# Sums over the states in batches of three column groups, in a selective-scan and attention kernel on one core

## The chip, the cores and the metric

The kernel runs on one core of one Trainium2 chip. The metric is the device time of one execution in microseconds (us); lower is better. In the trace the engines are PE (TensorE matmuls), PEld (TensorE weight loads, which overlap the matmuls), DVE (VectorE), ACT (ScalarE), POOL (GpSimd) and SP (the engine that issues the DMAs).

## The reference, cut to what matters

An input of 4 images x 16 x 16 x 192 goes through a state-space block, then linear attention, then an attention over 6 chosen heads of 12. The change touches only the scan of the first block:

```
def step(h, inp):                       # 256 steps in sequence
    u_t, d_t, B_t, C_t = inp            # per image and direction (4 directions)
    dA = jnp.exp(d_t[..., None] * As)   # 96 channels x 16 states
    h = h * dA + (d_t * u_t)[..., None] * B_t[:, :, None, :]
    y = jnp.einsum('bkcn,bkn->bkc', h, C_t)
    return (h, y)
```

The last line sums over the 16 states of each channel. The y of the four directions are then brought back to one order and added.

## The kernel before, in words

The 4 images are two halves of 2. A scan `n` (0 to 7) is one half in one direction. It has 96 channels x 16 states x 512 positions; 8 channels x 16 states fill the 128 partitions, so a scan is 12 **units** and the whole is 96 units (`SLOT_COUNT`). A unit `u` takes these steps, each engine in its own written order:

- PE, `spread_out(u)`: two bf16 matmuls (L1310 into `step_bc`, L1314 into `inp_bc`) spread the 8 channels over their 16 states each. There are two buffers of each. The first waits for the decay of unit u-2, the second for the scan of unit u-2.
- ACT, `expo(u)`, L690: the decay, from `step_bc`.
- DVE, `drive_of(u)`, L939, multiplies `inp_bc` by B, and `scan(u)`, L948, runs the recurrence into one of four `state` slots.
- POOL, `weigh(u)`, L528: `outp` = state x C, into one of three `outp` slots (`SLOTS`), so it waits for the sum of unit u-3 (`y_mm`).
- PE, `sum_states`, L1323: a float32 matmul with the 0/1 matrix `band` (128 x 96) adds the 16 states of each channel into `y_acc`, 96 x 512 in one PSUM bank. All 12 units of a scan accumulate into the same bank, each with zeros for the 88 channels that it does not hold. Each such matmul appears in the trace as two, so 96 sums are 192 rows.
- DVE, `add_y(n)`, L963, L966 or L973: at unit 3 of the next scan `y_acc` is added to `y_sum`; it waits for the sums of all 12 units.

PE's order in the loop at step u is `spread_out(u + 1)`, `sum_states(u - 3)`, then `pre` of a coming scan once in 12 steps (L1300), then the side products of the step. Side products are weight preparation in steps 14 to 42 and, from step 52 on, the attention work of the first half of the images, while the scans of the second half run (steps 48 to 95). After the last unit come `sum_states` of the last three units, `add_y(7)`, and then `rest`, the attention of what is left, which has no scan in it.

The stationary matrix of the sum is a window of `band`:

```
at = DI - GRP - GRP * g12
t_.matmul(y_acc[0:DI, :], band[:, at:at + DI], outp[:, u % SLOTS, :], ...)
```

Constants: `DI` 96, `GRP` 8, `UNITS` 12, `CHUNK` 32, `CHUNKS` 3, `PER_CHUNK` 4, `DIRS` 4.

Of the kernel before, what the change touches and what calls it, by code (L numbers as in the profile page):

```python
# [24 lines left out]
P = 128  # L25
# [4 lines left out]
TOK = IMG * L  # L30
TILES = TOK // P
CK = CH // 2
DI, NS, RANK, DIRS = 96, 16, 12, 4
GRP = P // NS
UNITS = DI // GRP
CHUNK = 32
CHUNKS = DI // CHUNK
PER_CHUNK = CHUNK // GRP
# [6 lines left out]
RING = 3  # L45
SLOTS = 3
STATE_SLOTS = 4
Y_LAG = 3
SOFTPLUS_LINEAR = 40.0
SERIES_BELOW = 0.0025  # L50
# [17 lines left out]
SLOT_COUNT = SCANS * UNITS  # L68
# [61 lines left out]
def products(step, n):  # L130

    if step in NO_PRODUCT:
        return []
    if step in WEIGHT_STEPS:
        return [step]
    if step[0] == "h" and step[1:].isdigit():
        j = int(step[1:])
        return [f"pt{n}{j - 2}"] * (1 < j <= TOPK + 1) + [f"pv{n}{j - 3}"] * (j > 2) + [f"s{n}{j}"] * (j < TOPK)
    return [f"{step}_{n}"]


def preparing(u, at):
# [27 lines left out]
def hybrid_kernel(nc, x, in_proj_w, conv_w, conv_b, x_proj_w, dt_w, dt_b, A_logs, Ds, norm_g, norm_b, out_proj_w,  # L170
# [5 lines left out]
    with ExitStack() as ctx:  # L176
        ctx.enter_context(nc.allow_non_contiguous_dma(reason="small parameter vectors"))

        def sb(name, shape, dt=F32):
            return ctx.enter_context(nc.sbuf_tensor(name, shape, dt))  # L180
# [30 lines left out]
        y_acc = ctx.enter_context(nc.psum_tensor("y_acc", [P, TOK], F32))  # L211
# [19 lines left out]
        band = sb("band", [P, 2 * DI - GRP])  # L231
# [44 lines left out]
        c_rep = sb("c_rep", [P, 2, TOK])  # L276
# [15 lines left out]
        n = TILES * CH  # L292
# [15 lines left out]
        decay = sb("decay", [P, SLOTS, IMG, L])  # L308

        state = sb("state", [P, STATE_SLOTS, TOK])  # L310
        outp = sb("outp", [P, SLOTS, TOK])
        y_sum = sb("y_sum", [DI, TOK])
        mst = sb("mst", [P, 4, TILES, 6])
        mv = sb("mv", [P, 4, TILES, 2])
# [122 lines left out]
        def _(pool):  # L437
            g = nc.gpsimd
# [14 lines left out]
            at = NS * (DI - GRP)  # L453
# [66 lines left out]
            def weigh(u):  # L520

                n, g12 = u // UNITS, u % UNITS
                if g12 == 0:
                    pool.wait_ge(S["c_there"], 16 * GRP * (n + 1))
                pool.wait_ge(S["state"], u + 1)
                if u >= SLOTS:
                    pool.wait_ge(S["y_mm"], u - SLOTS + 1)
                g.tensor_tensor(outp[:, u % SLOTS, :], state[:, u % STATE_SLOTS, :], c_rep[:, n % 2, :],  # L528
                                ALU.mult).then_inc(S["outp"], 1)

            def side(step, n):
# [37 lines left out]
        def _(act):  # L569
# [114 lines left out]
            def expo(u):  # L684

                act.wait_ge(S["bc_step"], u + 1)
                if u >= SLOTS:
                    act.wait_ge(S["state"], u - SLOTS + 1)
                at = u % (DIRS * UNITS)
                a.activation(decay[:, u % SLOTS, :, 1:L],  # L690
                             step_bc[u % 2][:, :].rearrange("p (b l) -> p b l", b=IMG)[:, :, 1:L],
                             ACT.Exp, scale=a_neg[:, at:at + 1]).then_inc(S["decay"], 1)
# [117 lines left out]
        def _(dve):  # L810
# [131 lines left out]
            def scan(u):  # L942

                dve.wait_ge(S["drive"], u + 1)
                dve.wait_ge(S["decay"], u + 1)
                if u >= STATE_SLOTS:
                    dve.wait_ge(S["outp"], u - STATE_SLOTS + 1)
                v.tensor_tensor_scan(state[:, u % STATE_SLOTS, :], decay[:, u % SLOTS, :, :].rearrange("p b l -> p (b l)"),  # L948
# [242 lines left out]
        def _(pe):  # L1191
            t_ = nc.tensor
# [109 lines left out]
            def spread_out(u):  # L1302

                n, g12 = u // UNITS, u % UNITS
                j, q = g12 // PER_CHUNK, g12 % PER_CHUNK
                if g12 == 0:
                    pe.wait_ge(S["stack"], 16 * 9 * (n + 1))
                if u >= 2:
                    pe.wait_ge(S["decay"], u - 1)
                t_.matmul(step_bc[u % 2][:, :], spread[:, q, :], stack[:, n % 2, j, 0:TOK], start=True, stop=True  # L1310
                          ).then_inc(S["bc_step"], 1)
                if u >= 2:
                    pe.wait_ge(S["state"], u - 1)
                t_.matmul(inp_bc[u % 2][:, :], spread[:, q, :], stack[:, n % 2, j, TOK:2 * TOK], start=True, stop=True  # L1314
                          ).then_inc(S["bc_inp"], 1)

            def sum_states(u):
                n, g12 = u // UNITS, u % UNITS
                pe.wait_ge(S["outp"], u + 1)
                if g12 == 0 and n > 0:  # L1320
                    pe.wait_ge(S["y_ev"], n)
                at = DI - GRP - GRP * g12
                t_.matmul(y_acc[0:DI, :], band[:, at:at + DI], outp[:, u % SLOTS, :],  # L1323
                          start=(g12 == 0), stop=(g12 == UNITS - 1)).then_inc(S["y_mm"], 1)

            def scores(n, j):
                p = n % IMG
# [181 lines left out]
            for u in range(SLOT_COUNT):  # L1509
                if u + 1 < SLOT_COUNT:  # L1510
                    spread_out(u + 1)
                if u >= Y_LAG:
                    sum_states(u - Y_LAG)
                if preparing(u, PRE_RAW):
                    pre(preparing(u, PRE_RAW))
                for item in beside[u]:
                    side(*item)
            for u in range(SLOT_COUNT - Y_LAG, SLOT_COUNT):
                sum_states(u)
            pe.wait_ge(S["y_ev"], SCANS)  # L1520
            for item in rest:
                side(*item)
# [29 lines left out]
```

## Time and profile before

| | |
|---|---|
| median of 3 runs | 508.72 us (507.52 to 510.63) |
| profiled execution, its own time | 506.69 us |
| span of its instructions | 504.8 us |
| busy: PE, DVE | 399.8 us (79%), 379.4 us (75%) |
| busy: POOL, ACT, PEld | 199.1 us, 182.3 us, 221.4 us |
| mean granted TensorE clock | 0.839 of full speed |

The scans run from about 50 to 328 us of the span. A busy share is of the whole span; the stretches differ, so it is read by stretch. A matmul's duration in the trace is that of the pipelined instruction; what it costs PE is the distance from its start to that of the next one.

### The profile page before, as it was taken

What the parts mean: (1) busy time and instruction counts of PE and PEld (TensorE: products, weight loads), DVE (VectorE), ACT (ScalarE), POOL (GpSimd) and SP (SyncE); (2) the same over time, 40 slices, a digit from 0 to 9 for tenths busy, and PEclk for the clock granted to TensorE, in tenths of its full rate; (3) what the DMA queues carried; (4) which work ended last, traced back from release to release, by engine and by line L of the source; (5) the groups of instructions that cost most, each with busy time, mean ns of one, the idle gap of its engine ahead of it and who ended that gap; (6) DMA issues with size and microseconds to landing.
All of it is one profiled execution on the core that took longest, in us unless ns stands there. A gap on an engine that the chain in (4) does not pass through costs nothing. (4 is left out here: it accounts for less than half of the span.)

```text
span 504.8 us, 5418 instructions
## 1 busy us (share of the span) xinstructions
PE 399.8 (79%) x1545; PEld 221.4 (44%) x1545; DVE 379.4 (75%) x732; ACT 182.3 (36%) x442; POOL 199.1 (39%) x199
## 2 busy tenths in 40 slices
PE   5511485878796856959999988999999999889882
PEld 4300121224232312415466465456665849676541
DVE  6354799998999999999789899885376364353574
ACT  2253443346463633522433323233324220334340
POOL 4414585658586866754454644510010010000011
PEclk9555787769897988857999999965999996958987
DMA  6403120110112111111010100000000000000000
GB/s 132 76 5 72 44 59 12 45 31 13 45 38 53 31 40 35 26 33 32 16 42 23 26 0 1 0 2 0 2 16 2 0 0 17 1 0 1 1 16 16
DMA packets 15742, 12.66 MB, mean 25 GB/s; under 512 B 7280, under 2 KB 11362, under 8 KB 15714
## 3 DMA queue, kind: packets, MB, share of 16 engines
q1 hardware_dynamic: 15713, 12.33, 10.6%
q8 instruction: 12, 0.20, 0.2%
q14 instruction: 17, 0.13, 0.1%
HBM read 2.62 MB, written 0.79 MB: 7 GB/s over the span
## 5 line engine op out<-in xcount | busy, mean ns | idle before, releaser
L528 POOL TENSOR_TENSOR outp<-state,c_rep 128x512 f32<-128x512 f32 x96 | 128.8, 1346 | 93.7 <-PE y_acc L1323 50.0
L948 DVE TENSOR_TENSOR_SCAN state<-decay,inp_bc 128x512 f32<-128x512 f32 x96 | 117.2, 1221 | 6.7 <-DVE inp_bc L939 3.2
L1323 PE MATMUL y_acc<-outp,band 128*96 128x512 f32 x192 | 114.1, 681 | 7.2 <-DVE y_sum L963 3.2
L690 ACT ACTIVATE decay<-step_bc,a_neg 128x510 f32<-128x510 f32 x96 | 64.9, 683 | 57.8 <-PE step_bc L1310 57.6
L939 DVE TENSOR_TENSOR inp_bc<-b_rep,inp_bc 128x512 f32<-128x512 f32 x96 | 65.4, 681 | 9.9 <-PE inp_bc L1314 9.8
L472 POOL TENSOR_TENSOR rs<-mv,neg_half 128x2 f32<-128x2 f32 x16 | 11.3, 706 | 152.0 <-DVE mv L984 149.8
L1314 PE MATMUL inp_bc<-stack,spread 96*128 96x512 bf16 x96 | 42.1, 439 | 36.6 <-DVE state L948 36.3
L1310 PE MATMUL step_bc<-stack,spread 96*128 96x512 bf16 x96 | 40.9, 426 | 16.9 <-DMA stack<-lo 14.3
L1323 PEld LDWEIGHTS y_acc<-outp,band 128*96 128x96 f32 x192 | 35.1, 187 | 24.3 <-issue 10.4
L1314 PEld LDWEIGHTS inp_bc<-stack,spread 96*128 96x128 bf16 x96 | 9.9, 103 | 78.2 <-DVE state L948 72.3
L1310 PEld LDWEIGHTS step_bc<-stack,spread 96*128 96x128 bf16 x96 | 10.5, 110 | 38.4 <-issue 30.3
L710 ACT ACTIVATE prob<-ring,nmaxs 128x256 f32<-128x256 f32 x24 | 11.1, 469 | 37.0 <-DVE nmaxs L1054 37.0
L678 ACT CAST hi<-step 96x512 bf16<-96x512 f32 x16 | 9.9, 616 | 33.4 <-DVE step L918 24.9
L518 POOL TENSOR_TENSOR lo<-step,mid 96x512 bf16<-96x512 f32 x16 | 19.4, 1232 | 3.4 <-ACT mid L682 3.4
L1411 PE MATMUL ring<-kvw,tT 96*128 96x480 f32 (+1 forms) x44 | 19.7, 570 | 0.0
L1062 DVE TENSOR_SCALAR prob<-prob,prec 128x256 f32<-128x256 f32 x48 | 16.7, 389 | 0.8
L1300 PE MATMUL ring<-room_g,pre_w 96*128 96x512 f32 x16 | 11.0, 780 | 7.5 <-DVE room_g L873 7.5
L1405 PE MATMUL ring<-tT,qw 96*128 96x256 f32 (+1 forms) x64 | 15.6, 386 | 0.0
L1405 PEld LDWEIGHTS ring<-tT,qw 96*128 96x128 f32 (+1 forms) x64 | 12.3, 194 | 5.3 <-issue 4.0
L682 ACT CAST mid<-step 96x512 bf16<-96x512 f32 x16 | 9.9, 616 | 13.1 <-DVE step L931 12.9
L867 DVE SCALAR_TENSOR_TENSOR room_e<-room_w,cw,room_e 96x544 f32<-96x544 f32 x16 | 14.2, 886 | 0.5
L511 POOL TENSOR_SCALAR sps<-spe 96x512 f32<-96x512 f32 x8 | 5.2, 652 | 23.6 <-ACT spe L669 23.6
(376 smaller groups left out, 709.4 us busy)
## 6 DMA issues: line engine op xcount, KB each, us to landing
b_rep<-bc SPq DMA_DIRECT2D x64, 32.0 KB, 2.0
c_rep<-bc SPq DMA_DIRECT2D x64, 32.0 KB, 2.0
stack<-hi SPq DMA_DIRECT2D x24, 64.0 KB, 2.0
stack<-mid SPq DMA_DIRECT2D x24, 64.0 KB, 2.0
stack<-lo SPq DMA_DIRECT2D x24, 64.0 KB, 2.0
x_tok<-in_x_dram SPq DMA_DIRECT2D x2, 384.0 KB, 3.8
out_dram<-room_g SPq DMA_DIRECT2D x4, 192.0 KB, 2.0
room_a<-in_L_attn_w_qkv_dram SPq DMA_DIRECT2D x1, 432.0 KB, 6.5
```

The source lines that it names most:

```text
L518: g.tensor_tensor(lo[:, i, :], step2[:, i, :], mid[:, i, :], ALU.subtract).then_inc(S["lo"], 1)
L528: g.tensor_tensor(outp[:, u % SLOTS, :], state[:, u % STATE_SLOTS, :], c_rep[:, n % 2, :], ALU.mult).then_inc(S["outp"], 1)
L690: a.activation(decay[:, u % SLOTS, :, 1:L], step_bc[u % 2][:, :].rearrange("p (b l) -> p b l", b=IMG)[:, :, 1:L], ACT.Exp, scale=a_neg[:, ...
L867: v.scalar_tensor_tensor(sums, window, cw[:, i:i + 1], sums, ALU.mult, ALU.add).then_inc(S["conv"], 1)
L939: v.tensor_tensor(inp_bc[u % 2][:, :], b_rep[:, n % 2, :], inp_bc[u % 2][:, :], ALU.mult).then_inc(S["drive"], 1)
L948: v.tensor_tensor_scan(state[:, u % STATE_SLOTS, :], decay[:, u % SLOTS, :, :].rearrange("p b l -> p (b l)"), inp_bc[u % 2][:, :], 0.0, AL ...
L1062: v.tensor_scalar(prob[p][:, m % 2, q, :], prob[p][:, m % 2, q, :], prec[p][:, m % 2, q:q + 1], None, ALU.mult).then_inc(S["prob_divided"] ...
L1310: t_.matmul(step_bc[u % 2][:, :], spread[:, q, :], stack[:, n % 2, j, 0:TOK], start=True, stop=True).then_inc(S["bc_step"], 1)
L1314: t_.matmul(inp_bc[u % 2][:, :], spread[:, q, :], stack[:, n % 2, j, TOK:2 * TOK], start=True, stop=True).then_inc(S["bc_inp"], 1)
L1323: t_.matmul(y_acc[0:DI, :], band[:, at:at + DI], outp[:, u % SLOTS, :], start=(g12 == 0), stop=(g12 == UNITS - 1)).then_inc(S["y_mm"], 1)
L1405: ins = t_.matmul(b_[:, u * L:(u + 1) * L], qw[0:CK + c, c, i * P:(i + 1) * P], tT[0:CK + c, c, at0:at0 + L], start=(c == 0), stop=(c == 1))
L1411: ins = t_.matmul(b_[:, 0:w], tT[0:CK + c, c, at:at + P], kvw[0:CK + c, c, j, :], start=(c == 0), stop=(c == 1))
```

## The change

A unit no longer takes the next 8 channels in order. Unit `u` of a scan takes group `j = u % 3` of 32 channels and within it the part `q`, so three units in succession belong to the three groups. The three units are summed together in every third step, and each sum writes only its own 32 rows of `y_acc` (partitions 0 to 31, 32 to 63 or 64 to 95), with a window of `band` of 32 columns. The batch for units 0 to 2 comes in step 5, that of units 3 to 5 in step 8, and so on; the last one follows the loop. `outp` has five slots. The column of `a_neg` that the decay uses follows the new order.

```diff
+OUT_SLOTS = 5
+def chunk_of(u):
+    return u % CHUNKS, u % UNITS // CHUNKS
...
-        outp = sb("outp", [P, SLOTS, TOK])
+        outp = sb("outp", [P, OUT_SLOTS, TOK])
...
-                if u >= SLOTS:
-                    pool.wait_ge(S["y_mm"], u - SLOTS + 1)
-                g.tensor_tensor(outp[:, u % SLOTS, :], state[:, u % STATE_SLOTS, :], c_rep[:, n % 2, :],
+                if u >= OUT_SLOTS:
+                    pool.wait_ge(S["y_mm"], u - OUT_SLOTS + 1)
+                g.tensor_tensor(outp[:, u % OUT_SLOTS, :], state[:, u % STATE_SLOTS, :], c_rep[:, n % 2, :],
...
-                at = u % (DIRS * UNITS)
+                j, q = chunk_of(u)
+                at = u // UNITS % DIRS * UNITS + j * PER_CHUNK + q
...
-                j, q = g12 // PER_CHUNK, g12 % PER_CHUNK
+                j, q = chunk_of(u)
...
-            def sum_states(u):
-                n, g12 = u // UNITS, u % UNITS
-                pe.wait_ge(S["outp"], u + 1)
-                if g12 == 0 and n > 0:
-                    pe.wait_ge(S["y_ev"], n)
-                at = DI - GRP - GRP * g12
-                t_.matmul(y_acc[0:DI, :], band[:, at:at + DI], outp[:, u % SLOTS, :],
-                          start=(g12 == 0), stop=(g12 == UNITS - 1)).then_inc(S["y_mm"], 1)
+            def sum_states(first):
+                pe.wait_ge(S["outp"], first + CHUNKS)
+                if first % UNITS == 0 and first > 0:
+                    pe.wait_ge(S["y_ev"], first // UNITS)
+                for u in range(first, first + CHUNKS):
+                    j, q = chunk_of(u)
+                    at = DI - GRP - GRP * q
+                    t_.matmul(y_acc[CHUNK * j:CHUNK * (j + 1), :], band[:, at:at + CHUNK], outp[:, u % OUT_SLOTS, :],
+                              start=(q == 0), stop=(q == PER_CHUNK - 1)).then_inc(S["y_mm"], 1)
...
-                if u >= Y_LAG:
-                    sum_states(u - Y_LAG)
+                if u % CHUNKS == CHUNKS - 1 and u >= Y_LAG:
+                    sum_states(u - Y_LAG - CHUNKS + 1)
...
-            for u in range(SLOT_COUNT - Y_LAG, SLOT_COUNT):
-                sum_states(u)
+            sum_states(SLOT_COUNT - CHUNKS)
```

## Rows read from the trace of the kernel before

**Rows 1.** Windows by stage: us, busy (instructions) by engine, PEclk, DMA.

```profile
57.00:108.00 51.00, 34.12 (x73) 11.02 (x74) 50.13 (x61) 18.80 (x32) 33.50 (x25) 0.79 0.16 39
108.00:120.00 12.00, 12.00 (x40) 5.75 (x39) 10.19 (x13) 8.53 (x17) 8.12 (x10) 0.76 0.07 16
120.00:228.00 108.00, 80.94 (x221) 29.55 (x220) 105.48 (x147) 48.07 (x85) 74.96 (x61) 0.85 0.16 38
228.00:330.00 102.00, 96.33 (x413) 56.15 (x412) 90.24 (x138) 34.44 (x79) 49.59 (x41) 0.97 0.07 16
330.00:505.00 175.00, 154.35 (x728) 106.18 (x728) 96.00 (x317) 51.66 (x191) 12.25 (x16) 0.84 0.02 5
```

**Rows 2.** Windows of 12 us in the stretch where PE is full, same columns.

```profile
228.00:240.00 12.00, 12.00 (x39) 7.09 (x38) 11.33 (x14) 3.66 (x6) 6.19 (x6) 0.78 0.10 24
240.00:252.00 12.00, 12.00 (x36) 5.58 (x35) 9.36 (x13) 5.52 (x11) 4.88 (x5) 1.00 0.07 16
252.00:264.00 12.00, 12.00 (x59) 8.16 (x58) 11.10 (x14) 3.58 (x9) 7.15 (x6) 1.00 0.20 44
264.00:276.00 12.00, 12.00 (x58) 7.66 (x57) 10.96 (x18) 4.61 (x9) 4.72 (x4) 1.00 0.08 19
276.00:288.00 12.00, 12.00 (x43) 5.97 (x41) 10.66 (x20) 3.74 (x8) 8.27 (x8) 1.00 0.13 33
288.00:300.00 12.00, 11.42 (x76) 8.00 (x75) 10.79 (x21) 3.94 (x10) 5.08 (x4) 1.00 0.00 0
300.00:312.00 12.00, 8.92 (x54) 5.35 (x54) 11.76 (x22) 3.47 (x13) 4.88 (x4) 1.00 0.00 1
312.00:324.00 12.00, 11.15 (x48) 6.59 (x47) 9.55 (x14) 4.90 (x13) 5.25 (x5) 1.00 0.00 0
324.00:330.00 6.00, 4.84 (x13) 1.74 (x14) 4.73 (x10) 1.02 (x4) 3.16 (x3) 1.00 0.00 0
```

**Rows 3.** The same windows for L1323 alone: PE and PEld busy, PEclk, DMA.

```profile
228.00:330.00 102.00, 38.02 (x72) 11.42 (x70) 0.97 0.07 16
```

**Rows 4.** Costliest groups: busy, mean ns, idle before, releaser.

```profile
L528 POOL TENSOR_TENSOR outp<-state,c_rep 128x512 f32<-128x512 f32 x96 | 128.8, 1346 | 93.7 <-PE y_acc L1323 50.0
L948 DVE TENSOR_TENSOR_SCAN state<-decay,inp_bc 128x512 f32<-128x512 f32 x96 | 117.2, 1221 | 6.7 <-DVE inp_bc L939 3.2
L1323 PE MATMUL y_acc<-outp,band 128*96 128x512 f32 x192 | 114.1, 681 | 7.2 <-DVE y_sum L963 3.2
L939 DVE TENSOR_TENSOR inp_bc<-b_rep,inp_bc 128x512 f32<-128x512 f32 x96 | 65.4, 681 | 9.9 <-PE inp_bc L1314 9.8
```

**Rows 5.** Chain of waits, pieces in order of time: start, us, what.

```profile
323.03 0.86 PE y_acc L1323 x2
...
384.98 0.98 PE ring L1349 x4
385.96 1.06 PE ring L1331 x4
```

**Rows 6.** Timeline at half clock: start, us, engine, line.

```profile
84.22 1.91 PE L1323 MATMUL y_acc<-outp,band 128*96 128x512 f32 x2
...
85.93 0.63 PE L1310 MATMUL step_bc<-stack,spread 96*128 96x512 bf16 x1
...
86.36 0.63 PE L1314 MATMUL inp_bc<-stack,spread 96*128 96x512 bf16 x1
```

**Rows 7.** Timeline at the end of the scans, same columns.

```profile
324.88 3.85 PE L1323 MATMUL y_acc<-outp,band 128*96 128x512 f32 x8
324.96 1.22 DVE L948 TENSOR_TENSOR_SCAN state<-decay,inp_bc 128x512 f32<-128x512 f32 x1
325.08 2.49 POOL L528 TENSOR_TENSOR outp<-state,c_rep 128x512 f32<-128x512 f32 x2
...
328.76 0.58 DVE L973 TENSOR_TENSOR y_sum<-y_sum,y_acc 96x256 f32<-96x256 f32 x1 [1.17 <-PE y_acc L1323]
```

**Rows 8.** One line of DVE: duration min/median/max, first and last start.

```profile
L931 DVE TENSOR_TENSOR step<-step,hi x16: 660/662/1450, 40.8 to 273.3; 96x512 f32<-96x512 f32 x16
```

**Rows 9.** Waits in the stretch of 228 to 330 us: total, times, longest.

```profile
POOL outp L528 <- PE y_acc L1323: 36.7, 21, 3.3
```

## The prediction

> **What bounds the kernel now.** I read the windows by stage first [rows 1], because the shares of the whole span hide that the limits differ. From 57 to 228 us (about 60 of the 96 units) DVE is busy 165.8 of 171 us, while PE is busy 127 of 171: DVE sets the pace, at 171/60 = 2.85 us a unit. From 228 to 330 us, where the attention work of the first half stands beside the last 36 units, PE is busy 96.3 of 102 us and DVE 90.2: there PE sets the pace most of the time. After 330 us there is no scan, and the change touches no instruction. The finer windows [rows 2] show how much room DVE leaves in the PE-bound stretch: DVE's idle time, 12 minus its busy time, is 0.67, 2.64, 0.90, 1.04, 1.34, 1.21, 0.24 and 2.45 us, and 1.27 in the last 6 us, in all 11.8 us. That is the most that any relief of PE can give in the scans, since no DVE work is removed. The costliest groups [rows 4] name PE's part in it: L1323 with 114.1 us busy. In the PE-bound stretch it has 38.0 us and 72 matmuls [rows 3], which are 36 sums or 12 batches of three.
>
> **The sum itself.** At full clock one sum takes PE 0.86 us, two matmuls of 0.43 [rows 5]; at half clock 85.93 - 84.22 = 1.71 us, two of 0.85 [rows 6]. I call one such matmul a slot. A batch of three sums is 6 slots one after another: 2.58 us. The change keeps 6 matmuls of 512 columns, narrows their output from 96 to 32 rows, and puts the three sums on different groups of rows. Narrowing alone gives nothing: four matmuls of L1349, 32 rows and 256 columns wide, take 0.98 us, and four of L1331, 128 rows and 256 columns, take 1.06 [rows 5]. A gain must come from sums of different groups running at the same time, and no row shows two such neighbours, so I bound it from both sides. Lower end: the three run fully side by side, 2 slots. Upper end: none overlaps, 6 slots. In between, if matmuls start only in written order and the second matmul of a sum must wait for the first, which uses the same rows, then the second of one sum can run only beside the first of the next: 4 slots. Going in and out of the narrow shape has a price too: the four slots of L1349 at 256 columns should take 4 x 0.213 = 0.85 us and take 0.98, the four of L1331 0.21 more; I take 0.2 a batch, between 0.1 and 0.35. So a batch costs 2 x 0.427 + 0.2 = 1.06 us, or 4 x 0.427 + 0.2 = 1.91, or 2.78, against 2.58.
>
> The Trainium skill bears on this. "TensorE: Matmul & The Clock Gate", Part 3, states that matmuls to different column tiles overlap and gives 2.38 times for three tiles of 512 columns; by that a batch would take 2.58/2.38 = 1.08 us, an estimate. The same part states that matmuls start and end in program order. By that the first case becomes the second, as worked out above from slots, since each float32 sum is two matmuls on one tile. "TensorEngine Tiling (Array Packing)", Key Properties, states that a change of tiling mode drains the engine; the 0.1 to 0.2 us at L1349 and L1331 agree with it. No run so far shows any overlap.
>
> **Part by part, against the profiled execution.**
>
> PE-bound stretch, 12 batches. With 4 slots each saves 0.67 us, 8.0 us in all or 0.94 per 12 us; it counts only as far as DVE has idle time, so window by window the smaller of the two: 0.67 + 0.94 + 0.90 + 0.94 + 0.94 + 0.94 + 0.24 + 0.94 + 0.47 = 7.0. With 2 slots it saves 1.52, or 2.1 per 12 us: 0.67 + 2.1 + 0.90 + 1.04 + 1.34 + 1.21 + 0.24 + 2.1 + 1.05 = 10.7. DVE does not become fully busy even where it is the bound; there about 0.2 us per 12 remain, so 1.7 us are taken off: gains of 5.3 and 9.0 us.
>
> DVE-bound stretch, 20 batches. The average load of PE falls, and that gives nothing. What can cost is the lump. In a batch step PE issues `inp_bc` of unit u+1 when scan u-1 ends, then the batch, then both spreads of u+2, and DVE wants the second of them two units later, on average 5.7 us. At full clock this path is 0.2 + 1.91 + 0.2 + 0.4 = 2.7 us and hidden. At half clock it is 0.43 + 3.42 + 0.2 + 0.43 + 0.63 = 5.1 us with 4 slots [slot lengths from rows 6]: just hidden, but in some 8 of the 20 steps a weight product or `pre` stands behind the batch, which adds 1.6 us at half clock and leaves DVE 1.0 us short. The granted clock of 0.79, 0.76 and 0.85 [rows 1] means half clock in about 35% of this stretch, so 8 x 1.0 x 0.35 = 2.8 at most; I take 1.2 us. With 2 slots: nothing.
>
> Moved and added waits. The first sum of a scan now stands two steps after `add_y`, so PE's waits for `y_sum` (3.2 us at L963, [rows 4]) go; where DVE or its cap is the bound this gives nothing more. `add_y` itself now waits for a batch in the same step in which the single sum stood; it is 1.0 us later with 4 slots, 0.2 with 2, and PE's work behind it goes on, so it costs only at the end. There the last `outp` is done at 325.08 + 2.49 = 327.57 us and DVE starts the last `add_y` 1.19 later, at 328.76 [rows 7], behind one sum; now behind three: +1.0 us with 4 slots, +0.2 with 2. The batch before it (units 90 to 92) fits ahead of that time. The index changes, the five slots and the column of `a_neg` cost nothing: same instructions, and the slot count for POOL lets it start earlier.
>
> POOL. Its 36.7 us of waiting for sums in the PE-bound stretch [rows 9] mostly vanish, so `weigh` starts right at the end of each scan instead of some 2 us later. POOL is no bound (busy 49.6 of 102). But a DVE instruction that reads only SBUF sometimes takes longer: L931 has 0.66 as median and 1.45 as its longest [rows 8], and in that instance POOL's L528 was running. With POOL moved, such meetings move too: +-2 us, taken at 0, because some of the present ones go.
>
> Sum with 4 slots: -5.3 + 1.2 + 1.0 = -3.1 us; with 2 slots: -9.0 + 0.2 = -8.8 us. The profiled execution is 506.7 us, 2.0 below the median of 508.7, so on the scale of the median: 505.6 and 499.9. **My forecast is that the groups overlap at least in part, and as no row leans to one end I take the middle of the two, -6 us, about 503.**
>
> **Rivals.**
> 1. *Written order halves the overlap* (4 slots): 505.6 us. For it: each sum is two matmuls on the same rows, which the 192 rows for 96 sums show. Against it: nothing in the trace. It is the upper part of my forecast, and it decides between a measurable gain and none.
> 2. *No overlap, and the lump stalls DVE*: slower. A batch is 2.78 us at full clock, 5.3 at half. PE-bound stretch: 12 x 0.2 = +2.4. DVE-bound stretch at half clock: 0.43 + 5.3 + 0.43 + 0.63 = 6.8 against 5.7, 1.1 x 20 x 0.35 = +7.7. End: +1.9. Together +12, 520.7 us, and about 514 if DVE catches up half of it. Its place is the start of DVE's L939 after each batch step; it decides from where a batch at half clock costs more than 5.7 - 1.5 = 4.2 us, about 5 slots. For it: no row of overlap, and L1349's 32-row matmuls save nothing by themselves.
> 3. *The clock takes it back*. A less loaded PE may be granted half clock in the PE-bound stretch, which now has 0.97 [rows 1]. One window of 12 us at 0.5 instead of 1.0 costs about 6 us there, since its products double: about 508.5 us, no change. Against it: with 2 slots PE still has over 80 of 102 us of work. The same place holds the meetings of POOL and DVE of above, if they turn out at +2 or worse.
>
> **How the numbers follow.** Overlap in part or in full 0.70, of which 4 slots 0.38 and 2 slots 0.32; no overlap 0.17; gain lost to clock or meetings 0.13. The range of 498 to 512 holds the first group nearly whole (499.9 and 505.6, each with about 2 us for the POOL meetings and the clock) and the third, and reaches towards rival 2; the overlap group alone would be 498 to 507.5. One per cent, about what a measurement of this kernel can tell from no change, is 5.1 us: faster is below 503.6, slower above 513.8. Faster: 0.30 of the 2-slot case, 0.13 of the 4-slot case, 0.03 of the rest, 0.46. Slower: most of rival 2 and a little of the third, 0.18. Within: 0.36.
>
> **What the profile after would show.** The distance from the start of a batch to PE's next instruction: 1.06, 1.9 or 2.8 us at full clock tells the slots at once. DVE's busy time in the last 36 units should rise towards 11.8 of 12. POOL's waits for `y_acc` should be near zero. In the first 60 units DVE's waits for `inp_bc` L1314 should stay near zero; if they appear at half clock, rival 2 or the lump of the 4-slot case is at work. The last `add_y` should start 1.4 us (2 slots) or 2.2 us (4 slots) after the last `outp`. The prediction would be wrong if PE's clock in the PE-bound stretch falls below 0.9, or if DVE's SBUF-only instructions grow by more than 2 us in total.

## The result, and the profile after

The changed kernel takes 523.49 us (median of 4 runs, 521.72 to 533.3) beside 509.68 for the kernel before on the same chip (4 runs): ratio 1.0274, interval 1.0205 to 1.0343. It is slower by about 14 us, where 503 had been forecast. Some executions of every version are a few per cent longer than the rest: medians here are over all runs, ratios over the fast ones alone, and as the execution profiled first was a slow one (533.3 us), the rows below are from a second profile of the same kernel, experiment e1. That execution took 524.18 us, span 522.3; the median of e1 over 4 runs is 522.5 (517.79 to 524.18), ratio 1.0266, interval 1.0203 to 1.033. The change adds lines, so numbers shift: L1332 is L1323 of the kernel before, L1321 is L1314, L946 is L939, L955 is L948 and L534 is L528.

The windows by stage answer to [rows 1]:

```profile
57.00:108.00 51.00, 28.81 (x70) 5.24 (x69) 48.61 (x57) 18.77 (x33) 33.23 (x25) 0.58 0.17 39
108.00:120.00 12.00, 8.54 (x17) 2.39 (x18) 11.42 (x15) 4.71 (x9) 6.41 (x9) 0.50 0.07 16
120.00:228.00 108.00, 72.66 (x233) 22.99 (x231) 101.22 (x141) 48.75 (x88) 74.14 (x62) 0.71 0.15 36
228.00:330.00 102.00, 90.56 (x383) 53.03 (x382) 87.59 (x130) 33.17 (x73) 48.16 (x38) 0.78 0.08 18
```

The column to read is PEclk: 0.79, 0.76 and 0.85 have become 0.58, 0.50 and 0.71, and in the PE-bound stretch 0.97 has become 0.78. PE is busy there for 90.56 us, only 5.8 less than before, and DVE for 87.59 us, where it had 90.24. As the scans of e1 end 13 us later, the window holds less of their work (383 matmuls of PE beside 413). The same work lies between the start of the recurrence (L948, here L955) of unit 60 and that of unit 95, the last; before, then e1:

```profile
215.18:324.96 109.78, 100.04 (x418) 57.52 (x419) 99.06 (x151) 36.31 (x80) 53.58 (x45) 0.92 0.08 20
222.34:338.05 115.71, 98.19 (x421) 56.83 (x421) 100.04 (x151) 35.95 (x80) 55.05 (x45) 0.79 0.08 19
```

At full clock 12 batches are some 19 us shorter than 36 single sums (12 x (2.58 - 0.99), the 0.99 from below). PE's busy time fell by 1.9 us, at a granted clock of 0.79 instead of 0.92.

The groups of PE that answer to [rows 4] and to its L1314:

```profile
L1332 PE MATMUL y_acc<-outp,band 128*32 128x512 f32 x192 | 50.7, 881 | 3.1 <-POOL outp L534 3.1
L1321 PE MATMUL inp_bc<-stack,spread 96*128 96x512 bf16 x96 | 48.4, 505 | 56.5 <-DVE state L955 56.2
```

The 192 matmuls of the sums keep PE busy for 50.7 us instead of 114.1, at the lower clock, so the relief is there, and larger than half. But L1321, which the change doesn't touch, has a mean of 505 ns, between the 0.38 and 0.63 us that single ones take at the two levels of the clock.

One batch at full clock and one at half clock, from the timeline of PE (start, us), answer to [rows 5, 6]:

```profile
249.12 0.38 PE L1321 MATMUL inp_bc<-stack,spread 96*128 96x512 bf16 x1
249.43 1.06 PE L1332 MATMUL y_acc<-outp,band 128*32 128x512 f32 x6
250.42 1.13 PE L1307 MATMUL ring<-room_g,pre_w 96*128 96x512 f32 x2
...
67.68 1.93 PE L1332 MATMUL y_acc<-outp,band 128*32 128x512 f32 x6
69.54 0.61 PE L1317 MATMUL step_bc<-stack,spread 96*128 96x512 bf16 x1
```

From the start of a batch to PE's next instruction are 250.42 - 249.43 = 0.99 us at full clock and 69.54 - 67.68 = 1.86 at half: three sums, six matmuls, in little more than the 0.86 and 1.71 us of one sum. The three groups of rows run side by side.

Where the time went is read from the starts of the recurrences on DVE, 12 units at a time; "last scan" is here the recurrence of unit 95. For before and for e1, in us:

| stretch | before | e1 | difference |
|---|---|---|---|
| span's start to first scan | 50.49 | 51.11 | +0.6 |
| units 0 to 11 | 36.4 | 37.1 | +0.7 |
| 12 to 23 | 37.8 | 41.8 | +4.0 |
| 24 to 59 (three times 12) | 27.1, 28.4, 35.1 | 27.4, 29.8, 35.1 | +1.8 |
| 60 to 83 (two times 12) | 40.6, 35.4 | 40.2, 36.7 | +0.9 |
| 84 to the last scan | 33.8 | 38.8 | +5.0 |
| last scan to the end | 179.8 | 184.3 | +4.5 |

Of the 5.0 us of the last twelve units 4.2 are one event: from the recurrence of unit 84 to the next pass 6.94 us, before 2.78. The timeline of e1 at this place (PE and DVE only; the last bracket is DVE's idle time before the instruction):

```profile
299.22 5.34 PE L1428 MATMUL ring<-v,room_a 128*128 128x34 f32 x24
299.24 1.22 DVE L955 TENSOR_TENSOR_SCAN state<-decay,inp_bc 128x512 f32<-128x512 f32 x1
...
304.78 0.63 PE L1321 MATMUL inp_bc<-stack,spread 96*128 96x512 bf16 x1
305.45 0.69 DVE L946 TENSOR_TENSOR inp_bc<-b_rep,inp_bc 128x512 f32<-128x512 f32 x1 [4.99 <-PE inp_bc L1321]
```

The attention product `cx` (24 matmuls, 5.34 us here, 2.76 before) runs at half clock; the `inp_bc` of the next unit is queued behind it, and DVE stands still for 4.99 us. In this event the chain is: half clock, a long product that no longer fits between two recurrences, an idle DVE.

The end of the scans in e1 answers to [rows 7]:

```profile
338.05 1.22 DVE L955 TENSOR_TENSOR_SCAN state<-decay,inp_bc 128x512 f32<-128x512 f32 x1
338.17 2.48 POOL L534 TENSOR_TENSOR outp<-state,c_rep 128x512 f32<-128x512 f32 x2
340.70 1.21 PE L1332 MATMUL y_acc<-outp,band 128*32 128x512 f32 x6 [3.07 <-POOL outp L534]
342.00 1.07 DVE L980 TENSOR_TENSOR y_sum<-y_sum,y_acc 96x256 f32<-96x256 f32 x2 [1.33 <-PE y_acc L1332]
```

The last `add_y` starts 342.00 - (338.17 + 2.48) = 1.35 us after the last product; before it was 1.19. POOL's waits from 228 to 330 us (total, times, longest), against [rows 9]:

```profile
POOL outp L534 <- DVE state L955: 29.3, 14, 5.6
POOL outp L534 <- PE y_acc L1332: 18.6, 7, 5.5
```

### The profile page after: what moved, and what is told of

It is laid out like the page before. It is cut to its first block and busy times, and to the rows that moved or that the text cites. A ratio compares the mean times of both kernels' runs of the same rounds, so it can differ in the third digit from the quotient of the medians.

```text
span 530.9 us, 5416 instructions
## 1 busy us (share of the span) xinstructions
PE 401.2 (76%) x1545; PEld 212.7 (40%) x1545; DVE 382.5 (72%) x732; ACT 181.5 (34%) x442; POOL 200.1 (38%) x199
## 3 DMA queue, kind: packets, MB, share of 16 engines
q1 hardware_dynamic: 15713, 12.33, 10.1%
## 5 line engine op out<-in xcount | busy, mean ns | idle before, releaser
L534 POOL TENSOR_TENSOR outp<-state,c_rep 128x512 f32<-128x512 f32 x96 | 130.4, 1364 | 103.4 <-DVE state L955 70.2
L955 DVE TENSOR_TENSOR_SCAN state<-decay,inp_bc 128x512 f32<-128x512 f32 x96 | 117.2, 1221 | 7.0 <-DVE inp_bc L946 3.8
L1321 PE MATMUL inp_bc<-stack,spread 96*128 96x512 bf16 x96 | 49.9, 520 | 56.0 <-DVE state L955 55.9
L946 DVE TENSOR_TENSOR inp_bc<-b_rep,inp_bc 128x512 f32<-128x512 f32 x96 | 65.4, 682 | 15.1 <-PE inp_bc L1321 15.1
L1317 PE MATMUL step_bc<-stack,spread 96*128 96x512 bf16 x96 | 48.5, 505 | 19.0 <-DMA stack<-lo 14.3
L1332 PE MATMUL y_acc<-outp,band 128*32 128x512 f32 x192 | 51.7, 898 | 3.1 <-POOL outp L534 3.1
L1321 PEld LDWEIGHTS inp_bc<-stack,spread 96*128 96x128 bf16 x96 | 10.5, 110 | 91.0 <-DVE state L955 85.0
L1317 PEld LDWEIGHTS step_bc<-stack,spread 96*128 96x128 bf16 x96 | 11.8, 123 | 47.9 <-issue 35.4
L1414 PE MATMUL ring<-tT,qw 96*128 96x256 f32 (+1 forms) x64 | 22.7, 518 | 0.0
L1307 PE MATMUL ring<-room_g,pre_w 96*128 96x512 f32 x16 | 14.1, 976 | 7.5 <-DVE room_g L880 7.5
L1414 PEld LDWEIGHTS ring<-tT,qw 96*128 96x128 f32 (+1 forms) x64 | 16.7, 266 | 6.5 <-issue 3.1
L1281 PE MATMUL ring<-room_j,room_a 96*96 96x384 f32 (+1 forms) x16 | 10.6, 763 | 5.6 <-DVE room_j L899 5.6
L664 ACT ACTIVATE step<-ring,dtb 96x512 f32<-96x512 f32 x8 | 5.5, 683 | 24.8 <-PE ring L1307 24.8
```

The costliest lines, as they stand in the source:

```text
L534: g.tensor_tensor(outp[:, u % OUT_SLOTS, :], state[:, u % STATE_SLOTS, :], c_rep[:, n % 2, :], ALU.mult).then_inc(S["outp"], 1)
L946: v.tensor_tensor(inp_bc[u % 2][:, :], b_rep[:, n % 2, :], inp_bc[u % 2][:, :], ALU.mult).then_inc(S["drive"], 1)
L1332: t_.matmul(y_acc[CHUNK * j:CHUNK * (j + 1), :], band[:, at:at + CHUNK], outp[:, u % OUT_SLOTS, :], start=(q == 0), stop=(q == PER_CHUNK - ...
L1414: ins = t_.matmul(b_[:, u * L:(u + 1) * L], qw[0:CK + c, c, i * P:(i + 1) * P], tT[0:CK + c, c, at0:at0 + L], start=(c == 0), stop=(c == 1))
```

## The experiments

The theory after the result: (A) a less loaded PE is granted a lower clock, and this takes the relief back. Rivals: (B) the lump, three sums in one step, delays `inp_bc`; (C) five slots let POOL start earlier, where its products run beside instructions of DVE on SBUF and one of the two is held up, called a meeting below; (D) the narrow form costs PE time of its own. The kernels first undo one part each.

**e1**, the changed kernel again. 

> The changed kernel again, for a profile beside the variants. The first profile had the three sums of a batch side by side (about 1.0 us a batch at full clock, 1.8 at half) but a granted clock of 0.54, 0.50, 0.71 and 0.73 where the kernel before had 0.79, 0.76, 0.85 and 0.97. Clock theory (PE has less to do in the scans, so the chip grants half clock for more of them, and the products there double): about 522 us, mean clock about 0.74. Lump theory (the batch and its wait for three outputs hold PE back, whatever the clock): the same time, but with PE standing in front of the batch or DVE waiting right after batch steps also where the clock is full.


Measured: 522.5 us, as above. Both theories had forecast this time, so it decides nothing between them.

**e2**, the batch with sums of 96 rows.

```diff
-                    at = DI - GRP - GRP * q
-                    t_.matmul(y_acc[CHUNK * j:CHUNK * (j + 1), :], band[:, at:at + CHUNK], ...
+                    at = DI - GRP - GRP * (PER_CHUNK * j + q)
+                    t_.matmul(y_acc[0:DI, :], band[:, at:at + DI], ...
```

> Order of the units, batches of three and five output slots as changed, but each sum writes all 96 rows again, so nothing runs side by side and PE has its old load. Clock theory: the clock comes back to about 0.84 and the time to 507 to 512 us. Lump theory: the lump is now 2.58 instead of 1.0 us long, so the time stays at 522 or goes above it.


Measured: 532.05 us (528.06 to 533.02, 4 runs), ratio 1.047 (1.0418 to 1.0523). The clock theory had forecast 507 to 512 us and missed: the clock did come back (0.82 and 0.90 in the two stretches, e1: 0.65 and 0.78), the time did not. So the lump without overlap is dear, and the overlap is worth 532.05 - 522.5 = 9.5 us against the same lump, at the clock that each is granted. DVE's waits in 57 to 350 us show the lump: 9.5 us for `inp_bc`, 6.5 for the softplus chain, whose product `pre` stands behind a batch, and 5.0 for `y_acc`.

**e3**, the narrow sums one at a time, a sum each step, five slots.

```diff
-                pe.wait_ge(S["outp"], first + CHUNKS)
+                pe.wait_ge(S["outp"], first + 1)
...
-                for u in range(first, first + CHUNKS):
+                for u in range(first, first + 1):
...
-                if u % CHUNKS == CHUNKS - 1 and u >= Y_LAG:
-                    sum_states(u - Y_LAG - CHUNKS + 1)
+                if u >= Y_LAG:
+                    sum_states(u - Y_LAG)
...
-            sum_states(SLOT_COUNT - CHUNKS)
+            for u in range(SLOT_COUNT - Y_LAG, SLOT_COUNT):
+                sum_states(u)
```

> Each sum writes its 32 rows, but alone, in the step in which the kernel before had it, so the sums take PE 2 slots each as before and only the width of the output is less. Clock theory by PE's busy time: clock and time as before, 508 to 512 us (plus up to 3 us for changing shape 96 times). Clock theory by the part of the array in use: the clock falls as in the changed kernel and the time is 518 us or more. Lump theory: as before, 508 to 512 us.


Measured: 521.96 us (518.79 to 529.38), ratio 1.0266 (1.0211 to 1.032), with a granted clock of 0.853 in the profile. No version of the theories had this pair: the lower time was forecast with a full clock, the higher one with a low clock. In this pair of kernels the clock goes with PE's busy time and not with the number of rows that a sum writes. The timeline of PE shows the price of the shape:

```profile
260.29 0.38 PE L1321 MATMUL inp_bc<-stack,spread 96*128 96x512 bf16 x1
260.60 1.05 PE L1332 MATMUL y_acc<-outp,band 128*32 128x512 f32 x2
261.57 1.19 PE L1428 MATMUL ring<-v,room_a 128*128 128x34 f32 x9
```

From `inp_bc` to the sum are 0.31 us, not the 0.22 that lie between two wide neighbours, and the pair takes 0.97 instead of 0.86: 0.2 us for going in and out of the narrow shape, 7 us over the 36 sums of the PE-bound stretch.

**e4**, the changed kernel with two repeated products a unit.

```diff
+                for _ in range(FILL):            # FILL = 2
+                    t_.matmul(step_bc[u % 2][:, :], spread[:, q, :], stack[:, n % 2, j, 0:TOK], start=True, stop=True)
                 t_.matmul(step_bc[u % 2][:, :], ...
```

> The changed kernel with two extra copies of the L1310 spread product in each unit, written to the same buffer just ahead of the real one and overwritten by it; this gives PE back 0.43 us a unit at full clock of the 0.53 that the change took, and nothing else. Clock theory: the clock rises towards 0.84 or above and the time falls well below 522, to 500 to 512 us, although PE does more. Lump theory: more work ahead of each decay, so 522 or slower.


Measured: 520.35 us (518.31 to 522.79), ratio 1.0257 (1.0207 to 1.0306): not to be told from e1. The filler brings the granted clock back to 0.81 before 228 us and to 0.90 behind it (e1: 0.65, 0.78), and it puts 2 x 0.22 = 0.44 us a unit on PE, of the 0.5 us that the batches had taken off. The clock was bought back with the time that had been saved. The forecast of the clock theory, 500 to 512 us, missed. And with nearly the load of the kernel before and most of its clock, e4 is still 12 us slower, so the clock can't be all of the loss: between the recurrences of units 60 and 95 it takes 114.6 us (e1 115.7, before 109.8) at a mean clock of 0.88 (0.79, 0.92).

**f1**, the kernel before with five output slots and nothing else; **f2**, the new order of units alone; **f3**, the changed kernel with three slots; **f4**, e3 with three slots.

```diff
 f1
-        outp = sb("outp", [P, SLOTS, TOK])
+        outp = sb("outp", [P, OUT_SLOTS, TOK])     # 5, in weigh and sum_states too
 f2: after.py with e3's loop, e2's matmul and OUT_SLOTS = 3
 f3: after.py with OUT_SLOTS = 3
 f4: e3 with OUT_SLOTS = 3
```

> The kernel before with five output slots in place of three and nothing else. In all variants with five slots DVE was busy 3 to 5 us longer on the same instructions, in those that read and write only SBUF. Meeting theory (POOL's product, no longer held back by the sums, meets these instructions of DVE and holds them up): DVE busy rises by 3 to 5 us over 379.4 and the time by 2 to 5 us, to 510 to 513. Clock theory alone: no change, 508.


Measured: 518.75 us (513.21 to 525.22, 6 runs) against 507.9, ratio 1.0209 (1.017 to 1.0248). More than either theory had allowed (508, or 510 to 513).

> The kernel before with the units in the new order (three groups in turn) and nothing else: single sums of 96 rows, three slots. Every theory: as before, 508 us, within 2.


Measured: 508.65 us (12 runs), ratio 1.0002 (0.9978 to 1.0025). The order costs nothing.

> The changed kernel with three output slots, so POOL waits for each batch and then makes three products in a row. Meeting theory: other meetings than with five slots, DVE busy nearer to 379 us, time 518 to 522. Lump theory: POOL stands still until each batch, scans are held by their own slots, slower than 523. Clock theory: as the changed kernel, 522, clock 0.74.


Measured: 530.7 us (529.99 to 531.11), ratio 1.0443 (1.0418 to 1.0467). With three slots POOL has to wait for the batch (108.3 us in 27 waits for `y_acc` over the run) and then computes three products in a row, beside which DVE is busy for 391.2 us, 11.8 more than before. Of the forecasts only that of the lump theory, slower than 523, holds. Beside e1 it also shows that the batch needs the slots: five of them are 8.2 us better than three here, where without a batch (f1) they are 10 us worse.

> Single sums of 32 rows in the old steps with three output slots: the narrow shape alone. The variant with five slots took 522 us and showed 0.21 us more per sum on PE at full clock (0.10 going in, 0.11 coming out). Switching theory: 36 sums in the stretch where PE is the bound x 0.2 = 7 us, little elsewhere, so 514 to 517 us, 3 to 5 below the one with five slots. If the meetings were the larger part, 510.


Measured: 514.55 us (514.39 to 525.56, 6 runs), ratio 1.0126 (1.01 to 1.0152). This is the shape alone: +6.6 us, near the 7 worked out under e3, so (D) holds for single sums; a batch pays it only once in three.

Put in a row, in medians: order +0.7, five slots +10.1 (f1 against f2), lump at full width +13.3 (e2 against f1), overlap -9.6 (e1 against e2), sum +14.5. These are steps along one path and not properties of the parts: f1 has the old order, and five slots are worth +10 without the batch and -8 with it.

The next four ask why slots cost, between a shift of buffers in SBUF and an earlier POOL.

```diff
 g1: before.py
-        outp = sb("outp", [P, SLOTS, TOK])
+        outp = sb("outp", [P, 5, TOK])             # three in use
 g2: after.py, g3: f1, g4: e4, each with
                 pool.wait_ge(S["state"], u + 1)
+                pool.wait_ge(S["bc_inp"], min(u + 2, SLOT_COUNT))
```

> The kernel before, with outp allocated for five slots but still rotated over three, so that only the places of the later buffers in SBUF change and no wait does. f1 with five slots in use cost 2.1%. Theory T (what costs is that POOL starts its product earlier, at the end of each scan, and so runs beside other DVE instructions): no change, 508 us, ratio 1.000. Rival L (the moved buffers cost): 516 to 519 us as in f1, ratio about 1.02.


Measured: 508.46 us (506.17 to 510.94, 12 runs), ratio 1.0018 (0.9994 to 1.0042). Not the places of the buffers.

> The changed kernel, with one more wait in weigh: POOL's product of unit u also waits for inp_bc of unit u+1, which PE issues just ahead of the place where the kernel before issued the sum that POOL waited for. So POOL is held back in the PE-bound stretch about as before, less one sum. Theory T: the 10.8 us that five slots cost in f1 come back at least in part, 512 to 515 us instead of 522.5, ratio about 1.01. Rival L: still 520 to 524, ratio 1.025, or above, as a later POOL makes the batches later. A second rival, that the lower clock is the larger part of the loss: also 520 to 524, with a granted clock of 0.74 to 0.78.


Measured: 526.54 us (525.09 to 537.02), ratio 1.0368 (1.0325 to 1.0412). Theory T missed, and the time is above the 520 to 524 of the other two, of which rival L had added "or above": worse than without the gate. A later POOL that makes the batches later would do this, but no row was read for it; the granted clock was 0.72.

> The kernel before with five slots in use, as f1, and the same wait of POOL for inp_bc of unit u+1. Theory T: back to 508 to 511 us, ratio 1.00 to 1.006. Rival L: 516 to 519 us, ratio 1.02.


Measured: ratio 1.0084 (1.004 to 1.0127); the 10 runs are spread over 509.48 to 525.32 us, median 516.28. By its ratio this looks like half a success of the gate, but the profile doesn't bear it out: the last scan starts at 330.44 us, in f1 at 330.23, and the granted clock of the scans is the same (0.87, 0.95). The gate changed nothing there. What differs between these two profiled executions, 509.7 and 517.3 us in span, lies at the very end, in stretches that neither kernel changes. f1:

```profile
474.00:486.00 12.00, 10.48 (x52) 6.02 (x51) 7.17 (x23) 5.74 (x22) 0.00 (x0) 1.00 0.00 0
486.00:498.00 12.00, 8.12 (x37) 4.32 (x36) 9.39 (x31) 5.25 (x18) 1.69 (x2) 1.00 0.05 16
```

and g3:

```profile
474.00:486.00 12.00, 10.48 (x33) 5.36 (x33) 4.58 (x14) 3.53 (x15) 0.00 (x0) 0.64 0.00 0
486.00:498.00 12.00, 11.95 (x38) 6.65 (x36) 7.28 (x24) 4.66 (x15) 0.92 (x2) 0.65 0.00 0
```

The first window has the same 10.48 us of PE's time for 52 matmuls in the one and 33 in the other: full clock against 0.64. That costs 186.9 - 179.5 = 7.4 us behind the last scan.

> The changed kernel with POOL's added wait of g2 and the two repeated spread products a unit of e4, which brought the granted clock from 0.74 to 0.78 up to 0.81 to 0.85. If the meetings and the clock each carry a part and add up, this is the sum of both: 522.5 - 2 (e4) - 8 to 10 (g2 by theory T) = 510 to 512 us, ratio about 1.006. If neither carries it, 520, ratio 1.025.


Measured: 526.42 us (520.74 to 533.54), ratio 1.0315 (1.0261 to 1.0369). That is above both forecasts (510 to 512, and 520). The parts don't add up to a gain; with g2 this ended the idea that a held-back POOL repairs the change.

The last four ask where the slots' time lies, and whether relief of PE has any worth.

```diff
 h1: f1 again, for a second profile
 h2: before.py, h3: f1, each with
+                w = TOK if g12 == 0 else TOK // 4
-                t_.matmul(y_acc[0:DI, :], band[:, at:at + DI], outp[:, u % SLOTS, :],
+                t_.matmul(y_acc[0:DI, 0:w], band[:, at:at + DI], outp[:, u % SLOTS, 0:w],
 h5: e4
-                for _ in range(FILL):
+                for _ in range(FILL if u < 60 else 0):
```

> The kernel of f1 once more (the kernel before with five output slots), for a second profile. If the five slots cost in the scans, the last scan starts at 330 us as in f1's and g3's profiles and what varies is the part behind it: 179.5 us with PE at full clock about 150 us behind the last scan, 187 us with half clock there. If the slots' cost lies elsewhere, the scans end 5 us or more later than 330 in a run of 516 us or more.


Measured: 525.3 us in one execution, span 523.5. The last scan starts at 333.73 and the rest takes 189.8 us: the span is 13.8 us longer than in f1's profile, of the same kernel. 10.3 us more lie behind the scans, and 4.5 in the last twelve units, where the event of e1 stands again:

```profile
300.40 0.70 DVE L940 TENSOR_TENSOR inp_bc<-b_rep,inp_bc 128x512 f32<-128x512 f32 x1 [4.54 <-PE inp_bc L1315]
```

So that event needs no batch and no narrow rows, and no relief of PE either; half clock at this place is enough: in f1's profile, the same program with full clock there, the wait is 0.69 us.

> The kernel before, with 11 of every 12 sums cut to a quarter of their 512 columns (so three quarters of the columns lack all but the first unit's sum). Order, waits, slots and the 96 rows are as before; PE is relieved by about 0.6 us a sum, 20 us in the last 36 units, the same as by the overlapped batches. If relief of PE is worth what the prediction said for 2 slots: -9, about 499 us, ratio 0.982, last scan 9 us earlier. If the clock takes it back: a granted clock of 0.75 to 0.80 against 0.84 to 0.88, and 506 to 510 us.


Measured: 515.52 us (one run at 507.41, the other five from 515.30 to 516.86) against 508.44 (shortest run 506.7). The forecast for worthwhile relief had been 499, that of the clock theory 506 to 510. Whether it is slower at all can't be said from two groups of runs; that it isn't faster can. The granted clock is low in all six, 0.72 to 0.78. Its windows by stage:

```profile
57.00:108.00 51.00, 28.58 (x72) 11.81 (x72) 49.87 (x57) 20.24 (x35) 34.59 (x26) 0.57 0.17 40
108.00:120.00 12.00, 8.66 (x24) 4.17 (x24) 11.74 (x15) 5.89 (x11) 6.41 (x9) 0.53 0.07 17
120.00:228.00 108.00, 69.05 (x231) 34.48 (x229) 103.39 (x143) 48.60 (x87) 76.95 (x62) 0.67 0.16 37
228.00:330.00 102.00, 92.85 (x410) 66.31 (x410) 90.29 (x135) 34.55 (x78) 48.21 (x39) 0.76 0.07 17
```

These are the clearest rows of the study. Order, waits, slots, rows and step of every sum are those of the kernel before; only PE's work is less, by some 20 us in the last stretch. The clock falls to 0.57, 0.53, 0.67 and 0.76, PE is busy for 92.85 us instead of 96.33, and DVE does 90.29 us of work where it did 90.24. From the recurrence of unit 60 to that of unit 95 h2 takes 110.8 us (331.34 - 220.56), 1.0 more than before, where 9 less had been forecast. So (A) is shown for the clock, and for the gain that did not come, without the help of any other part of the change.

The same trace, unit by unit against before, shows how. From unit 65 to unit 71, where both have full clock but for the first microsecond, h2 takes 16.5 us instead of 19.8: while the clock stays, relief does count. Units 73, 74 and 84, at half clock in the main, then lose 3.9 us. The largest piece, 2.4 us in unit 84, is the event of e1, with neither batch nor five slots:

```profile
295.50 5.17 PE L1420 MATMUL ring<-v,room_a 128*128 128x34 f32 x24
301.56 0.69 DVE L939 TENSOR_TENSOR inp_bc<-b_rep,inp_bc 128x512 f32<-128x512 f32 x1 [3.26 <-PE inp_bc L1314]
```

Another 2.4 us go in units 71 and 81, and not by the clock: there instructions of DVE on SBUF last longer, L909 1.40 us and the two of L991 0.95, with a product of POOL beside them. f1 and e1 lose the same 2.3 us in these two units. L909 before, then in h2 with POOL's product:

```profile
253.26 1.09 DVE L909 SCALAR_TENSOR_TENSOR spl<-spe,spl 96x512 f32<-96x512 f32 x1
...
255.36 2.49 DVE L909 SCALAR_TENSOR_TENSOR spl<-spe,spl 96x512 f32<-96x512 f32 x1
256.04 1.27 POOL L528 TENSOR_TENSOR outp<-state,c_rep 128x512 f32<-128x512 f32 x1
```

The units from 87 on gain 1.9 us again, which leaves the 1.0.

> The same short sums with five output slots. If relief is worth its 9 us and the slots cost 10.8 as in f1: 510 us. If the clock takes the relief back: 518 us, ratio 1.02. If the slots cost because POOL starts earlier, they cost nothing here beyond h2, as with short sums POOL no longer waits long for a slot in either kernel: h3 equals h2.


Measured: 514.5 us (510.26 to 522.47, 12 runs), ratio 1.0102 (1.0064 to 1.014), clock 0.717 to 0.784. Neither 510 nor 518; by the medians five slots add nothing to h2, but both spread too widely to say more. In its profile units 60 to 95 take 108.5 us, 1.3 less than before.

> The changed kernel with two repeated spread products a unit in units 0 to 59 alone, where DVE sets the pace. If the low clock there makes the scans late (half-clock batches and weight products in the steps of 2.85 us): 516 to 518 us, since e4's filler is kept where it helps and left out where it costs PE time. If the clock of the last 36 units matters instead: 522 as the changed kernel. e4, with filler in all units, had 520.4.


Measured: 522.23 us (518.57 to 527.15), ratio 1.0241 (1.0198 to 1.0285): the changed kernel's time. Clock 0.78 before 228 us and 0.77 behind it. In its first 60 units it gains 2.4 us on e1, and the last twelve take 38.8 us as there. The forecast by a lower clock in the first 60 units, 516 to 518 us, missed. That the clock of the last 36 units decides instead is not shown: e4, which has it back at 0.90, takes 38.6 us for the same twelve.

The mean granted clock of all profiled executions in the two stretches goes with PE's load:

| kernels | PE's load | 57 to 228 us | 228 to 330 us |
|---|---|---|---|
| before, g1, f1 and h1, f2, f4, g3, e3, e2 | full-length sums, one after another | 0.82 to 0.87 | 0.90 to 0.98 |
| e4, g4 | overlapped sums and filler | 0.81, 0.78 | 0.90, 0.88 |
| h5 | overlapped sums, filler in the first 60 units | 0.78 | 0.77 |
| the changed kernel (first profile and e1), f3, g2 | overlapped sums | 0.61 to 0.65 | 0.73 to 0.78 |
| h2, h3 | short sums | 0.63 | 0.76, 0.80 |

No version is faster than the kernel before.

## Why the prediction was wrong

**The bound.** Right as a reading of the state before, wrong as a base for a sum. That PE sets the pace in the last 36 units assumed that its work has a fixed length.

**The sum itself.** The overlap was foreseen, with 4 slots as the likelier case; what came is the 2 slots: 0.99 us a batch at full clock, or 1.08 with the 0.09 that PE takes longer going in, where 1.06 had been worked out. Written order doesn't halve the overlap, though each sum is two matmuls on the same rows; rivals 1 and 2 fall, as far as they rest on missing overlap. The rule of the Trainium skill that gives 2.38 times for three column tiles ("TensorE: Matmul & The Clock Gate", Part 3) agrees with this trace: 2.58/1.08 is 2.4, and 2.58/0.99 is 2.6. The other rule of that part, on starts and ends in program order, is not contradicted by these rows, but it does not cost the 4 slots that the prediction worked out beside it. The 0.2 us for the shape was right too (0.2 in e3).

**The PE-bound stretch**, forecast -9.0 us, is the step that failed. Between the starts of scan 60 and the last scan e1 takes 40.2 + 36.7 + 38.8 = 115.7 us against 109.8, +5.9. The failed assumption is the one beside rival 3, that "PE still has over 80 of 102 us of work" and so keeps its clock; it had 90.56 and was granted 0.78. (With 2 slots the prediction's own numbers give less than 80: 96.3 - 12 x 1.52 = 78.1.) Rival 3's mechanism is what the runs showed, and its price for one window, about 6 us, was fair (4.2 for the event at 299 us). Its extent was not: one window of 12 us had been counted, and 0.78 means half clock in (1 - 0.78)/0.5 = 44% of 102 us. h2, with this clock and no other part of the change, has +1.0 us in place of the -9: what full clock gave in some units went back at half clock (3.9 us) and in the meetings of DVE with POOL (2.4). Rival 3 had been given 0.13, for no change; how the other 5 us of e1 divide among clock, lump and slots is not shown. The event of unit 84 is half clock in e1 and in h1 (39.1 us for the last twelve units), but e4 takes as long there with half clock only from 310 to 320 us, in five waits of DVE for `inp_bc`, of which three (1.44, 0.65 and 1.87 us) stand at full clock.

**The DVE-bound stretch**, nothing forecast for 2 slots: +6.5 us in the first 60 units. It isn't the stall that had been feared in the place where it had been feared; from unit 1 on, DVE's waits for `inp_bc` L1321 are all behind 299 us. But the lump does reach DVE by another way, the softplus chain, whose product `pre` stands behind a batch:

```profile
74.40 1.93 PE L1332 MATMUL y_acc<-outp,band 128*32 128x512 f32 x6
...
76.26 2.08 PE L1307 MATMUL ring<-room_g,pre_w 96*128 96x512 f32 x2
...
79.09 0.42 DVE L912 TENSOR_SCALAR spl<-step 96x512 f32<-96x512 f32 x1 [1.59 <-ACT step L664]
```

Besides a first one near 54 us that all these versions have, e1 has three such waits in this stretch, 2.9 us in all, at half clock in the main. The kernel before has none, nor has h2 with the low clock but no lump, nor e4 with the lump and a clock of 0.81. Of the rest, 2.4 us are more work of DVE in units 12 to 23, in SBUF-only instructions beside POOL, and 1.3 a longer wait of L886 for its input from ACT (3.38 us at half clock, 2.09 before).

**POOL.** "Taken at 0" was wrong, and so was "the five slots cost nothing". The same DVE instruction in g1 and in f1, with POOL's beside it:

```profile
117.61 0.83 DVE L905 TENSOR_SCALAR spl<-step 96x512 f32<-96x512 f32 x1
118.11 1.47 POOL L528 TENSOR_TENSOR outp<-state,c_rep 128x512 f32<-128x512 f32 x1
```

```profile
119.61 2.08 DVE L906 TENSOR_SCALAR spl<-step 96x512 f32<-96x512 f32 x1
120.11 1.29 POOL L529 TENSOR_TENSOR outp<-state,c_rep 128x512 f32<-128x512 f32 x1
```

Both pairs start 0.50 us apart in the records. In g1 DVE is through in 0.83 us and POOL's product is the longer one; in f1 DVE lasts until 121.69, 0.3 us beyond POOL's end. The Trainium skill ("SBUF — State Buffer", "SBUF: two separate sides") calls the port pair of the two an exclusive lock for a whole instruction, which goes to the one that starts first. These rows agree in that one lasts until about the other's end; they don't bear out the second half as recorded: in both pairs DVE's start is the first, and only in f1 is DVE held up. DVE's busy time over the whole run is 3.1 us above before's 379.4 in e1, 5.3 in f1 and 11.8 in f3. But f2, with three slots, has 2.5 as well and costs nothing in its median, and its units 12 to 23 take the same 40.2 us as f1's. So f1 has some 3 us more of such meetings than f2, not ten, and they don't explain the difference of the medians.

**Behind the scans** nothing had been forecast, since no instruction changes: +4.5 us in e1. In the profiles of this kernel family this part has anything from 179.1 us (f2, mean clock 0.85) to 190.8 us (the first profile of the changed kernel, 0.80). So the end of the scans can move and the total by more or less than that.

**The signs.** Right: the batch's length; no waits for `inp_bc` in the first 60 units; the last `add_y` 1.35 us after the last product (1.4). Wrong: DVE busy for 10.3 of 12 us in 228 to 330 us, not near 11.8; POOL's waits for `y_acc` halved (18.6 us), not gone. Both conditions under which the prediction called itself wrong came true: the clock below 0.9, and SBUF-only work of DVE up by more than 2 us.

**Left open.** Why five slots alone move f1's median by 10 us. Three profiles put 3.5 to 9 us of it before the last scan (330.23, 330.44 and 333.73 us against 324.96 and 326.72 for before and g1) and 0 to 10 behind it, at half clock; but f2's profile has its last scan at 329.74 as well. That the slots make half clock behind the scans more likely is what the medians suggest, and no run here shows the way in which they would. How much of e1's 14.5 us each of lump, slots and clock would carry alone can't be told either, since they act through the same clock: the differences between the medians are known to about 3 us each.

## What to carry to other kernels

Before counting relief of PE as time, read its granted clock in that stretch and ask what the engine does with less work: here about two thirds of the sums' work was removed twice, by overlap and by leaving columns out, and each time the clock fell and most of the gain went back with it. A cheap check is the second of these: cut the columns of the matmuls that an idea would save, change nothing else, and see if the kernel becomes faster at all. And more slots for a buffer are a change of timing, to be tried alone.

## What the runs showed of the hardware

- Three groups of float32 sums, each two matmuls on 32 rows of their own, issued one sum after the other, take 0.99 us at full clock and 1.86 at half; one sum of 96 rows takes 0.86 and 1.71.
- A single sum in the narrow shape costs about 0.1 us on the way in and 0.1 on the way out (e3), +6.6 us for 96 sums (f4).
- With the sums' load cut to a third, the mean granted clock fell from 0.83 to 0.63 or 0.65 in 57 to 228 us, and from 0.97 to 0.76 or 0.78 in 228 to 330 us, though PE was busy there for 90 us and more of 102 (e1, h2; e2, with batches of full sums, had 0.82 and 0.90).
- The same program had 179.5 and 189.8 us behind its last scan in two executions (f1, h1), with half clock in other windows; a single profile doesn't tell the time of this kernel to better than 10 us.
- A DVE instruction on SBUF of 0.83 us (g1) took 2.08 (f1) beside a POOL product, at the same distance of their starts in the records; another of 1.09 us (before) took 2.49 (h2).
